# A graph layer with a gated update: layer norm of the second group on two engines, and a new order of work between the first and the second group

## Chip, core and metric

The kernel runs on one core of one Trainium2 chip, in one launch. The metric is the device time in microseconds (us). Engines are named as in the profile: PE is TensorE (PEld its weight loads), DVE is VectorE, ACT is ScalarE, POOL is GpSimd, and SP is SyncE, which here only issues transfers.

## What is computed

The inputs are 64 graphs of 128 nodes with 128 features and a 128x128 adjacency each. Cut to what matters:

```python
h = maximum(layernorm(x), 0)                       # per node
c = relu(bn1(conv1(h)))                            # 1x1 convolution over the nodes
x_conv = relu(bn2(conv2(c)) + h)                   # 17 taps, 128 -> 128 channels
s = h @ w_se.T + b_se                              # 3 numbers for each node
A = exp(-|s_n - s_m|^2) * adj
x_nmp = A @ relu(h @ w_msg.T + b_msg)              # messages, gathered
gi = concat([x_conv, x_nmp]) @ w_ih.T + b_ih       # gates r, z, n
gh = h @ w_hh.T + b_hh
r, z = sigmoid(gi_r + gh_r), sigmoid(gi_z + gh_z)
out = x + (1 - z) * tanh(gi_n + r * gh_n) + z * h
```

## The kernel before

The 64 graphs are worked on in 8 groups `g` of 8 graphs. A group has 1024 columns (8 graphs of 128 nodes), cut into two chunks `c` of 512. All products are float32 made of three matmuls on split numbers (`three`, lines 1016 to 1019: high times high, low times high, high times low); the high half of each operand is written by ACT, the low half by DVE. The 17 taps are done as nine smaller convolutions, `sub_conv(g, 0)` to `sub_conv(g, 8)`, on derived inputs `v_hi` and `v_lo` and on derived weights `wt_hi` and `wt_lo`, which the kernel makes itself during group 0 in 13 lots (`lot_high` on ACT, `lot_low` on DVE, line 694). Lot 12 holds the input weights of the gates.

There is no scheduler: each engine has one list of calls written by hand, and the engines meet at semaphores. The work of neighbouring groups is interlocked, and from group 1 on the lists are a loop. The order between groups 0 and 1 is written out. The names that matter there:

- Layer norm: `ln_stats(g)` (DVE, line 674, eight instructions) and `moments(g)` (line 681), then `ln_scale(g)` on POOL (lines 330 to 335: four small instructions, of which the power at 333 gives `rstd`), then `ln_rows(g)` on ACT (line 422, eight instructions, one a graph). For group 0 alone the split form is used: `ln_first` and `hn_rows_first` on DVE with four of the graphs (lines 706, 711, 714), `ln_scale_first` on POOL (324, only the power), and `ln_rows_first` on ACT with the other four (396).
- `h_transpose(g, c)` (PE, line 1036) turns the rows into `h`; ACT writes `h_hi` and `hf` (`h_rows`, 432 and 433) and DVE `h_lo` (`h_low`, 701). `by_graphs` (414) stores `h` once more, for the messages.
- `conv1` (PE), `conv1_rows` (ACT, 441, writes `cp`), and from `cp` on DVE `level2_b` (738), `level1`, `v_low_b`, `level2_u` and `v_low_u`.
- `messages(g)` on PE (1060 and 1063), on ACT (487 to 494). In the form for group 1 it uses PSUM banks 0 to 2 and so waits for `conv1_rows(1, 0)`, which empties bank 2. From its three numbers a node, `distances` makes `slots` (on POOL for every group but the first, lines 247 to 266), `factor_transposes` (PE, 1074), `factor_rows` (ACT, 500), `distance` (PE, 1087), `exponent` (ACT, 506) and `masked` (DVE, 819) follow, and last `gather` (PE, 1097), whose result ACT and DVE split into `n_hi` (514) and `n_lo` (825).
- Convolution results: `m_shared(g, i)` (ACT, 478) empties PSUM bank 0 after sub-convolutions 0, 3 and 6; the next of these on PE waits for it. `join_b`, `add_h`, `add_shared`, `join_y` (DVE, 776, 786, 797, 805) add up `y`, and `xc_high` (ACT, 520) and `xc_low` (DVE, 812) split it.
- Gates: `gates_h(g, c)` (nine matmuls on `h`, into banks 3, 4 and 6), `gates_in(g, c)` (nine on the gathered messages `n`, nine on `xc`). `ghn_rows` (526), `reset_rows` (532), `update_rows` (537), `candidate` (568) on ACT, `reset` (831, 835) and `update` (840 to 850) on DVE. In `gates_h(g, 1)` the part of gate z waits until `update_rows(g, 0)` has read bank 6:

```python
three(bank(4), HH(R), *h, True, False)
if c:
    pe.wait_ge(z_ready, NCH * g + 1)
three(bank(6), HH(Z), *h, True, False)
```

SP loads the rows `xin` of the next group once the last layer norm has read the buffer, then `xt`, stores the output, and loads the mask; it has one queue and waits in this order.

## Time and profile before

| | us |
|---|---|
| median of 3 runs | 298.87 |
| lowest and highest | 298.52, 299.6 |
| the profiled execution, its own time | 298.59 |
| its span, first to last instruction | 296.8 |
| PE busy in the span | 285.9 (96%) |
| DVE, ACT, POOL busy | 225.7, 185.9, 65.6 |

The span leaves 1.8 us of the execution's time outside it. The granted clock of PE is 0.998 of full speed over the span. In the rows below, a row of a timeline has the start, the duration, the engine, the line, what it writes and reads, and in brackets the idle time before it and what ended that. Durations of matmuls overlap: a matmul with 512 columns lasts some 0.40 us in the rows, while the next one starts about 0.23 us after it.

### The profile page before, as it was taken

The page shows a single profiled execution, that of the slowest core. Times are in us where ns is not written, and L with a number is a line of the kernel's source. Part 1 is how long each engine was busy: PE and PEld are TensorE (multiplying, and loading weights), DVE is VectorE, ACT ScalarE, POOL GpSimd, SP SyncE. Part 2 cuts the span into 40 slices and gives each one's busy share as a digit, 9 for nine tenths or more (in the row PEclk, how much of TensorE's full clock was granted, in tenths as well). Part 3 has the DMA queues.
Part 4 walks back from the last instruction along what each step waited for, and adds up shares of the span by engine and source line. Part 5 has one row for each costly group of instructions (what it writes and reads, how often), then busy time and mean ns, then how long its engine had stood idle before and what let it go on. Part 6 is the DMA issues. An engine that isn't in the chain of part 4 may idle for free.

```text
span 296.8 us, 5432 instructions
## 1 busy us (share of the span) xinstructions
PE 285.9 (96%) x1943; PEld 259.1 (87%) x1943; DVE 225.7 (76%) x497; ACT 185.9 (63%) x355; POOL 65.6 (22%) x129
## 2 busy tenths in 40 slices
PE   8999888999999999999999999999999999999993
PEld 6699866899889998899889998899988998899993
DVE  5988967986679668796598776796587966786556
ACT  3795479658656677548757567647666586561354
POOL 6300130750015300550005500351005500130000
PEclk9999999999999999999999999999999999999999
DMA  7700111044000610035000620017000420013001
GB/s 254 278 3 0 35 51 58 0 144 145 0 0 3 227 59 0 0 110 176 2 0 0 183 103 1 2 35 249 1 2 1 141 73 0 3 22 122 0 1 71
DMA packets 6798, 18.96 MB, mean 64 GB/s; under 512 B 882, under 2 KB 1268, under 8 KB 6772
## 3 DMA queue, kind: packets, MB, share of 16 engines
q1 hardware_dynamic: 6624, 18.62, 19.0%
q8 instruction: 15, 0.25, 0.4%
q14 instruction: 11, 0.09, 0.1%
q10 hardware_dynamic: 148, 0.01, 0.0%
HBM read 14.43 MB, written 4.19 MB: 63 GB/s over the span
## 4 chain that ended last, share of the span: by engine, by line
PE 84%; DVE 7%; ACT 4%; POOL 2%; issue 1%; DMA 1%; DVEq 0%; ACTq 0%; POOLq 0%
PE ps L1017 23%; PE ps L1019 22%; PE ps L1018 22%; PE ps L1063 4%; PE ps L1097 4%; PE ps L1201 3%; PE ps L1036 2%; DVE wt_lo L694 2%; PE ps L1060 1%; PE ps L1074 1%; ACT wt_hi L390 1%; PE ps L1087 1%; ACT cp L441 1%; DMA out<-gate 1%; DVE stats L674 1%
## 5 line engine op out<-in xcount | busy, mean ns | idle before, releaser
L1017 PE MATMUL ps<-v_hi,wt_hi 128*128 128x256 f32 x320 | 92.8, 290 | 2.0 <-DVE v_lo L754 0.8
L1019 PE MATMUL ps<-v_hi,wt_lo 128*128 128x256 f32 x320 | 90.1, 281 | 0.0
L1018 PE MATMUL ps<-v_lo,wt_hi 128*128 128x256 f32 x320 | 89.7, 280 | 0.0
L1017 PEld LDWEIGHTS ps<-v_hi,wt_hi 128*128 128x128 f32 x320 | 60.2, 188 | 3.5 <-issue 2.7
L1018 PEld LDWEIGHTS ps<-v_lo,wt_hi 128*128 128x128 f32 x320 | 60.4, 189 | 0.3
L1019 PEld LDWEIGHTS ps<-v_hi,wt_lo 128*128 128x128 f32 x320 | 60.1, 188 | 0.0
L247 POOL CAST slots<-s_sb 128x48 fp32r<-128x48 f32 x7 | 2.2, 311 | 147.9 <-ACT s_sb L489 147.9
L422 ACT ACTIVATE hn<-xin,nmr,rstd 128x128 f32<-128x128 f32 x56 | 22.3, 482 | 14.7 <-POOL nmr L335 14.7
L1017 PE MATMUL ps<-h_hi,wt_hi 128*128 128x512 f32 (+1 forms) x67 | 26.2, 391 | 0.0
L1019 PE MATMUL ps<-h_hi,wt_lo 128*128 128x512 f32 (+1 forms) x67 | 25.8, 386 | 0.0
L1018 PE MATMUL ps<-h_lo,wt_hi 128*128 128x512 f32 (+1 forms) x67 | 25.8, 385 | 0.0
L797 DVE TENSOR_TENSOR y<-y,mbs 128x512 f32<-128x512 f32 x16 | 11.0, 690 | 15.6 <-ACT mbs L478 15.4
L1017 PE MATMUL ps<-n_hi,wt_hi 128*128 128x512 f32 (+1 forms) x51 | 20.1, 394 | 1.2 <-DVE wt_lo L694 1.2
L805 DVE SCALAR_TENSOR_TENSOR y<-ps,par,y 128x256 f32<-128x256 f32 x32 | 14.9, 482 | 8.1 <-PE ps L1019 7.1
L1018 PE MATMUL ps<-n_lo,wt_hi 128*128 128x512 f32 (+1 forms) x51 | 19.5, 383 | 0.0
L1018 PE MATMUL ps<-xc_lo,wt_hi 128*128 128x512 f32 (+1 forms) x51 | 19.5, 383 | 0.0
L1019 PE MATMUL ps<-n_hi,wt_lo 128*128 128x512 f32 (+1 forms) x51 | 19.5, 382 | 0.0
L1019 PE MATMUL ps<-xc_hi,wt_lo 128*128 128x512 f32 (+1 forms) x51 | 19.5, 382 | 0.0
L1017 PE MATMUL ps<-xc_hi,wt_hi 128*128 128x512 f32 (+1 forms) x51 | 19.4, 380 | 0.0
L812 DVE SCALAR_TENSOR_TENSOR xc_lo<-y,xc_hi 128x512 fp32r<-128x512 f32 x16 | 10.3, 688 | 10.2 <-ACT xc_hi L520 10.2
L526 ACT ACTIVATE gn<-ps,par 128x512 f32<-128x512 f32 x15 | 10.4, 691 | 11.8 <-PE ps L1019 11.7
L514 ACT ACTIVATE n_hi<-ps 128x512 fp32r<-128x512 f32 x16 | 9.6, 599 | 13.0 <-PE ps L1097 13.0
(152 smaller groups left out, 647.9 us busy)
## 6 DMA issues: line engine op xcount, KB each, us to landing
mask<-adj_t SPq DMA_DIRECT2D x8, 512.0 KB, 3.3
xt<-x_t SPq DMA_DIRECT2D x8, 512.0 KB, 4.1
out<-gate SPq DMA_DIRECT2D x15, 256.0 KB, 4.1
xin<-x_nm SPq DMA_DIRECT2D x7, 512.0 KB, 3.8
w<-w_conv SPq DMA_DIRECT2D x1, 576.0 KB, 6.0
gate<-w_gate SPq DMA_DIRECT2D x1, 576.0 KB, 7.0
xin<-x_nm SPq DMA_DIRECT2D x2, 256.0 KB, 3.0
w<-w_conv SPq DMA_DIRECT2D x1, 512.0 KB, 5.0
```

The source lines that it names most:

```text
L422: last = act.activation(hn[:, j, :], xin[:, j, :], ACT.Identity, bias=nmr[:, j:j + 1], scale=rstd[:, j:j + 1])
L514: act.activation(n_hi[:, :, 4 * c:4 * c + 4], bank(src).rearrange("p (b n) -> p n b", n=P), ACT.Copy).then_inc(n_hi_ready, 1)
L526: act.activation(gn[c][:], bank(3), ACT.Identity, bias=par[:, HN:HN + 1], scale=0.5).then_inc(ghn_ready, 1)
L797: dve.tensor_tensor(y_at(s), y_at(s), mbs[1 + s][:].rearrange("p (l b) -> p l b", b=GB).unsqueeze(2).broadcast_to([P, QUART, 2, GB]), ALU. ...
L805: dve.scalar_tensor_tensor(out=at, in0=quarter(1 + t), scalar=par[:, SC2:SC2 + 1], in1=at, op0=ALU.mult, op1=ALU.add).then_inc(y_ready, 1)
L812: dve.scalar_tensor_tensor(out=xc_lo[:, cols(c)], in0=y[:, cols(c)], scalar=0.0, in1=xc_hi[:, cols(c)], op0=ALU.max, op1=ALU.subtract).the ...
L1017: pe.matmul(dst, wt_hi[:, blk, :], hi, start=start, stop=False)
L1018: pe.matmul(dst, wt_hi[:, blk, :], lo, start=False, stop=False)
L1019: return pe.matmul(dst, wt_lo[:, blk, :], hi, start=False, stop=stop)
L1063: last = pe.matmul(ps[:, first + k, i * MW:(i + 1) * MW], hg[:, 3 * k + i, :], w_a[:, P:P + MW], start=False, stop=i == count - 1)
L1097: last = pe.matmul(ps[:, dst, i * P:(i + 1) * P], msg[:, b, :], aff[:, b, :], start=True, stop=True)
L1201: pe.matmul(bank(4), idle[:, 0:P], idle[:], start=True, stop=True)
```

## The change

The layer norm of group 1 takes the split form that only group 0 had: DVE writes `vpe`, POOL makes only the power, DVE writes `nmr` and normalizes four graphs, ACT the other four. The helpers get the group as an argument, with waits for the last readers of their buffers. The lists between the groups are reordered:

- PE: `gates_in` becomes `gates_n` and `gates_xc`. `gates_h(0, 1)` comes ahead of the transposes of group 1, `gates_n(0, 1)` behind them and ahead of `conv1`, `messages(1)` ahead of `gates_xc(0, 1)`. In group 1, `factor_transposes` and `distance` come two sub-convolutions later.
- DVE: lot 12 and `n_low` come ahead of the `join_y` calls, `moments(1)` behind them. `update(0, 0)` comes ahead of `h_low(1, 0)`. `ln_stats(2)` moves up from the loop to behind `h_low(1, 1)`. At the head of group 1, `join_b` and `add_h` come ahead of `update(0, 1)`.
- ACT: `reset_rows(0, 0)`, then the four rows of layer norm, then `update_rows(0, 0)` and `candidate(0, 0)`, all ahead of `h_rows(1)`. `ghn_rows(0, 1)` comes behind `conv1_rows(1)`. In group 1, `m_shared(1, 0)` comes ahead of `factor_rows(1)`.

Groups 2 to 7 keep their order.

```diff
@@ -280,8 +281,8 @@
                 if g + 1 < NG:
 
                     sp.wait_ge(hn_ready, NCH * (g + 1))
-                    if g == 0:
-                        sp.wait_ge(hn_first, 1)
+                    if g < 2:
+                        sp.wait_ge(hn_first, g + 1)
                     sp.dma_start(xin[:], x_nm[g + 1]).then_inc(x_landed, 16)
 
                 upto(sp, sum_ready, NCH * g)
@@ -319,19 +320,24 @@
             pool.memset(slots[:, 0, :, 14:16].bitcast(F32), 1.0).then_inc(pool_set, 1)
             pool.memset(slots[:, 1, :, 12:14].bitcast(F32), 1.0).then_inc(pool_set, 1)
 
-            def ln_scale_first():
-                pool.wait_ge(vpe_first, 1)
+            def ln_scale_first(g):
+                pool.wait_ge(vpe_first, g + 1)
+
+                upto(pool, hn_ready, NCH * g)
+                upto(pool, hn_first, g)
                 pool.tensor_tensor(rstd[:], vpe[:], neg_half[:], ALU.pow).then_inc(rstd_first, 1)
 
             def ln_scale(g):
                 pool.wait_ge(mv_ready, g + 1)
 
                 upto(pool, hn_ready, NCH * g)
+                if g == 2:
+                    pool.wait_ge(hn_first, 2)
                 pool.tensor_scalar(vpe[:], mv[:, :, 1], EPS, None, ALU.add).then_inc(pool_ln, 1)
                 pool.tensor_scalar(nmean[:], mv[:, :, 0], -1.0, None, ALU.mult).then_inc(pool_ln, 1)
-                pool.wait_ge(pool_ln, 3 * g - 1)
+                pool.wait_ge(pool_ln, 3 * (g - 1) - 1)
                 pool.tensor_tensor(rstd[:], vpe[:], neg_half[:], ALU.pow).then_inc(pool_ln, 1)
-                pool.wait_ge(pool_ln, 3 * g)
+                pool.wait_ge(pool_ln, 3 * (g - 1))
                 pool.tensor_tensor(nmr[:], nmean[:], rstd[:], ALU.mult).then_inc(rstd_ready, 1)
 
             def two(i):
@@ -358,12 +364,13 @@
 
             pool.wait_ge(pool_set, 5)
             affine_power()
-            ln_scale_first()
+            ln_scale_first(0)
             affine()
-            for g in range(NG):
-                if g + 1 < NG:
-                    ln_scale(g + 1)
-                    distances(pool, g + 1)
+            ln_scale_first(1)
+            distances(pool, 1)
+            for g in range(2, NG):
+                ln_scale(g)
+                distances(pool, g)
 
         @block.scalar
         def _(act):
@@ -389,9 +396,11 @@
                     act.wait_ge(wg_landed, 16)
                 act.activation(wt_hi[:, first:first + count, :], source, ACT.Copy).then_inc(wt_hi_ready, 1)
 
-            def ln_rows_first():
-
-                act.wait_ge(rstd_ready, 1)
+            def ln_rows_first(g):
+
+                act.wait_ge(rstd_ready, g + 1)
+
+                upto(act, ht_ps, NCH * g)
                 for j in range(4, GB):
                     last = act.activation(hn[:, j, :], xin[:, j, :], ACT.Identity, bias=nmr[:, j:j + 1],
                                           scale=rstd[:, j:j + 1])
@@ -572,7 +581,7 @@
             act.wait_ge(row_ready, 2)
             act.activation(row[0:1, :], row_raw[0:1, :], ACT.Copy).then_inc(row_split, 1)
             act.activation(row_hi[32:33, :], row_raw[32:33, :], ACT.Copy).then_inc(row_split, 1)
-            ln_rows_first()
+            ln_rows_first(0)
             h_rows_first()
             lot_high(1)
             lot_high(2)
@@ -606,17 +615,17 @@
             act.wait_ge(pool_par, 8)
             ghn_rows(0, 0)
             xc_high(0)
-            ln_rows(1)
             reset_rows(0, 0)
+            ln_rows_first(1)
             update_rows(0, 0)
+            candidate(0, 0)
             h_rows(1, 0, 0)
             h_rows(1, 1, 1)
-            candidate(0, 0)
             by_graphs(1, 0, 0)
             by_graphs(1, 1, 1)
-            ghn_rows(0, 1)
             conv1_rows(1, 0, 2)
             conv1_rows(1, 1, 7)
+            ghn_rows(0, 1)
             v_high_b(1, 0)
             v_high_b(1, 1)
             messages(1)
@@ -627,8 +636,12 @@
                 ahead = g + 1 < NG
                 update_rows(g - 1, 1)
                 candidate(g - 1, 1)
-                factor_rows(g)
-                m_shared(g, 0)
+                if g == 1:
+                    m_shared(g, 0)
+                    factor_rows(g)
+                else:
+                    factor_rows(g)
+                    m_shared(g, 0)
                 exponent(g)
                 if ahead:
                     ln_rows(g + 1)
@@ -701,13 +714,16 @@
                 dve.tensor_tensor(h_lo[g % 2][:, cols(c)], hf[g % 2][:, cols(c)], h_hi[g % 2][:, cols(c)],
                                   ALU.subtract).then_inc(h_lo_ready, 1)
 
-            def ln_first():
-                dve.wait_ge(mv_ready, 1)
+            def ln_first(g):
+                dve.wait_ge(mv_ready, g + 1)
                 dve.tensor_scalar(vpe[:], mv[:, :, 1], EPS, None, ALU.add).then_inc(vpe_first, 1)
 
-            def hn_rows_first():
-
-                dve.wait_ge(rstd_first, 1)
+            def hn_rows_first(g):
+
+                dve.wait_ge(rstd_first, g + 1)
+
+                upto(dve, ht_ps, NCH * g)
+                upto(dve, hn_ready, NCH * g)
                 dve.scalar_tensor_tensor(out=nmr[:], in0=mv[:, :, 0], scalar=-1.0, in1=rstd[:], op0=ALU.mult,
                                          op1=ALU.mult).then_inc(rstd_ready, 1)
                 for j in range(4):
@@ -893,14 +909,14 @@
                 last = stats_of(0, j)
             last.then_inc(stats_ready, 1)
             moments(0)
-            ln_first()
+            ln_first(0)
             lot_low(0)
             dve.wait_ge(row_split, 2)
             dve.wait_ge(row_landed, 32)
             dve.tensor_tensor(row[32:33, :], row_raw[32:33, :], row_hi[32:33, :], ALU.subtract).then_inc(row_split, 1)
             dve.wait_ge(w2a_landed, 16)
             dve.tensor_tensor(fb[:, 0:4, :], w2[:, 0:8:2, :], w2[:, 1:8:2, :], ALU.add).then_inc(sums_ready, 1)
-            hn_rows_first()
+            hn_rows_first(0)
             dve.wait_ge(w2b_landed, 16)
             dve.tensor_tensor(fb[:, 4:8, :], w2[:, 8:16:2, :], w2[:, 9:16:2, :], ALU.add).then_inc(sums_ready, 1)
             dve.wait_ge(sums_ready, 2)
@@ -941,19 +957,22 @@
             masked(0, 0)
             masked(0, 1)
             lot_low(11)
-            moments(1)
             add_shared(0, 1)
-            join_y(0, 1, 0)
+            lot_low(12)
             n_low(0, 0, 5)
             n_low(0, 1, 7)
+            join_y(0, 1, 0)
             join_y(0, 1, 1)
-            lot_low(12)
+            moments(1)
+            ln_first(1)
             xc_low(0, 0)
             xc_low(0, 1)
+            hn_rows_first(1)
             reset(0, 0)
+            update(0, 0)
             h_low(1, 0)
             h_low(1, 1)
-            update(0, 0)
+            ln_stats(2)
             level2_b(1, 0)
             level2_b(1, 1)
             level1(1)
@@ -965,13 +984,20 @@
             reset(0, 1)
             for g in range(1, NG):
                 ahead = g + 1 < NG
-                if ahead:
-                    ln_stats(g + 1)
+                if g == 1:
                     moments(g + 1)
-                update(g - 1, 1)
-                join_b(g, 0)
-                join_b(g, 1)
-                add_h(g)
+                    join_b(g, 0)
+                    join_b(g, 1)
+                    add_h(g)
+                    update(g - 1, 1)
+                else:
+                    if ahead:
+                        ln_stats(g + 1)
+                        moments(g + 1)
+                    update(g - 1, 1)
+                    join_b(g, 0)
+                    join_b(g, 1)
+                    add_h(g)
                 masked(g, 0)
                 masked(g, 1)
                 add_shared(g, 0)
@@ -1019,8 +1045,8 @@
                 return pe.matmul(dst, wt_lo[:, blk, :], hi, start=False, stop=stop)
 
             def h_transpose(g, c, dst):
-                if g == 0 and c == 0:
-                    pe.wait_ge(hn_first, 1)
+                if g < 2 and c == 0:
+                    pe.wait_ge(hn_first, g + 1)
                 else:
                     pe.wait_ge(hn_ready, NCH * g + c + 1)
                 if g == 1:
@@ -1144,9 +1170,8 @@
                     pe.wait_ge(z_ready, NCH * g + 1)
                 three(bank(6), HH(Z), *h, True, False)
 
-            def gates_in(g, c):
+            def gates_n(g, c):
                 nm = [n[:, c * HALF:(c + 1) * HALF, :] for n in (n_hi, n_lo)]
-                xc = (xc_hi[:, cols(c)], xc_lo[:, cols(c)])
                 if c == 0:
                     pe.wait_ge(n_lo_ready, NCH * g + NCH)
                     if g == 0:
@@ -1156,6 +1181,9 @@
                     pe.wait_ge(v_ready, NCH * g + 1)
                 three(bank(5), IH(N, 1), *nm, True, False)
                 three(bank(6), IH(Z, 1), *nm, False, False)
+
+            def gates_xc(g, c):
+                xc = (xc_hi[:, cols(c)], xc_lo[:, cols(c)])
                 pe.wait_ge(xc_lo_ready, NCH * g + c + 1)
                 three(bank(4), IH(R, 0), *xc, False, True).then_inc(r_ps, 1)
                 if g < NG - 1:
@@ -1228,22 +1256,30 @@
             gather(0, 0, 5)
             gather(0, 1, 7)
             gates_h(0, 0, True)
-            gates_in(0, 0)
+            gates_n(0, 0)
+            gates_xc(0, 0)
+            gates_h(0, 1, True)
             h_transpose(1, 0, 0)
             h_transpose(1, 1, 1)
-            gates_h(0, 1, True)
+            gates_n(0, 1)
             conv1(1, 0, 2)
             conv1(1, 1, 7)
             messages(1)
-            gates_in(0, 1)
+            gates_xc(0, 1)
             for g in range(1, NG):
                 ahead = g + 1 < NG
                 sub_conv(g, 0)
-                factor_transposes(g)
+                if g > 1:
+                    factor_transposes(g)
                 sub_conv(g, 1)
-                distance(g)
+                if g > 1:
+                    distance(g)
                 sub_conv(g, 2)
+                if g == 1:
+                    factor_transposes(g)
                 sub_conv(g, 3)
+                if g == 1:
+                    distance(g)
                 sub_conv(g, 4)
                 sub_conv(g, 5)
                 gather(g, 0, 5)
@@ -1259,11 +1295,13 @@
                 if ahead:
                     conv1(g + 1, 0, 0)
                     conv1(g + 1, 1, 7)
-                gates_in(g, 0)
+                gates_n(g, 0)
+                gates_xc(g, 0)
                 if ahead:
                     gates_h(g, 1, ahead)
                     messages(g + 1)
-                    gates_in(g, 1)
+                    gates_n(g, 1)
+                    gates_xc(g, 1)
                 else:
                     for p in (1, 2):
                         part_gates_h(p)
```

## Rows read from the trace of the kernel before

**Rows 1.** Busy time by stretch: stretch, its length, busy us (instructions) by engine, clock, DMA.

```profile
36.00:57.00 21.00, 18.70 (x98) 15.13 (x98) 16.48 (x29) 17.49 (x36) 7.38 (x11) 1.00 0.16 51
...
90.00:124.00 34.00, 34.00 (x236) 31.08 (x235) 25.97 (x57) 21.92 (x42) 8.08 (x16) 1.00 0.19 63
```

**Rows 2.** Timeline of PE from group 0 to group 1: start, duration, instruction, idle time.

```profile
38.24 0.40 PE L1019 MATMUL ps<-h_hi,wt_lo 128*128 128x512 f32 x1
39.81 0.47 PE L1017 MATMUL ps<-n_hi,wt_hi 128*128 128x512 f32 x1 [1.17 <-DVE wt_lo L694]
...
44.10 1.03 PE L1036 MATMUL ps<-ident,hn 128*128 128x128 f32 x8
44.89 0.48 PE L1017 MATMUL ps<-h_hi,wt_hi 128*128 128x512 f32 x1
...
49.82 0.75 PE L1060 MATMUL ps<-row,ones 128*128 128x396 f32 x3 [1.13 <-ACT cp L441]
...
52.12 0.48 PE L1017 MATMUL ps<-n_hi,wt_hi 128*128 128x512 f32 x1
...
58.55 0.66 PE L1074 MATMUL ps<-ident,slots 128*128 128x128 f32 x4 [0.21 <-POOL slots L266]
```

**Rows 3.** Timeline of PE in group 1: the first gather and sub-convolution 6.

```profile
67.80 1.05 PE L1097 MATMUL ps<-aff,msg 128*128 128x128 f32 x8
...
69.04 0.36 PE L1017 MATMUL ps<-v_hi,wt_hi 128*128 128x256 f32 x1
```

**Rows 4.** Timeline of DVE, group 0 first, then from group 0 to group 1.

```profile
8.04 1.11 DVE L714 TENSOR_SCALAR hn<-xin,mv,rstd 128x128 f32<-128x128 f32 x4
...
35.41 0.64 DVE L681 BATCH_NORM_AGGREGATE mv<-stats 128x2 f32<-128x6 f32 x8
...
37.13 1.28 DVE L825 TENSOR_TENSOR n_lo<-ps,n_hi 128x512 fp32r<-128x512 f32 x2
...
38.72 0.95 DVE L694 TENSOR_TENSOR wt_lo<-gate,wt_hi 128x768 fp32r<-128x768 f32 x1
39.58 1.29 DVE L812 SCALAR_TENSOR_TENSOR xc_lo<-y,xc_hi 128x512 fp32r<-128x512 f32 x2
...
47.58 0.69 DVE L840 TENSOR_TENSOR gate<-hf,gn 128x512 f32<-128x512 f32 x1
...
50.47 0.78 DVE L738 TENSOR_TENSOR vtb<-cp 128x264 f32<-128x264 f32 x2 [0.27 <-ACT cp L441]
...
58.05 1.64 DVE L674 BATCH_NORM_STATS2 stats<-xin 128x6 f32<-128x128 f32 x8
```

**Rows 5.** Timeline of ACT from group 0 to group 1.

```profile
38.84 1.15 ACT L520 ACTIVATE xc_hi<-y 128x512 fp32r<-128x512 f32 x2 [0.81 <-DVE y L805]
39.89 3.19 ACT L422 ACTIVATE hn<-xin,nmr,rstd 128x128 f32<-128x128 f32 x8
...
44.30 0.69 ACT L537 ACTIVATE gate<-ps,par 128x512 f32<-128x512 f32 x1 [0.65 <-PE ps L1019]
...
48.93 1.50 ACT L441 ACTIVATE cp<-ps,par 128x512 f32<-128x512 f32 x2
...
68.12 0.45 ACT L478 ACTIVATE mbs<-ps,par 128x256 f32<-128x256 f32 x1
```

**Rows 6.** Timeline of POOL: the power for group 1 and for group 2.

```profile
37.14 1.67 POOL L333 TENSOR_TENSOR rstd<-vpe,neg_half 128x8 f32<-128x8 f32 x1
...
61.73 1.95 POOL L333 TENSOR_TENSOR rstd<-vpe,neg_half 128x8 f32<-128x8 f32 x1
63.76 1.22 POOL L335 TENSOR_TENSOR nmr<-nmean,rstd 128x8 f32<-128x8 f32 x1
```

**Rows 7.** Transfers: SP's issue of group 2's rows, and issues by kind with us to landing.

```profile
43.10 0.33 SPq L285 DMA_DIRECT2D xin<-x_nm  x1
...
xin<-x_nm SPq DMA_DIRECT2D x1, 512.0 KB, 3.4
...
gate<-w_gate SPq DMA_DIRECT2D x1, 576.0 KB, 7.0
```

## Prediction

> **What bounds the kernel now.** I read the busy times by stretch first. In a stretch of the steady loop PE is busy for all of 34.00 us; between the groups 0 and 1 it is busy 18.70 of 21.00 us, so 2.30 us are idle [rows 1]. The reader is to see that PE sets the time, that the change touches no matmul, and that nothing can be won but PE's idle time in the one place that the change edits. Then PE's timeline there: 1.17 us before the n gates, for the weights of lot 12; 1.13 us before `messages(1)`, for `cp`; and 0.21 us before the factor transposes, for `slots` [rows 2]. What a stall costs is best read from starts. The 512-column matmuls start every 0.234 us: from 38.24 the next would start at 38.47, and started at 39.81, 1.34 late. The first one behind a stall or a switch takes 0.32 to the next, 0.08 more. `messages(1)` starts at 49.82; the six matmuls of `conv1` end their slots at 48.54, so 1.28 are lost. Fifteen matmuls of 256 columns at 0.118 take 1.78, so `sub_conv(1, 0)`, which starts at 52.12 + 0.32 + 17 x 0.234 = 56.42, is done at 58.18; the transposes at 58.55 are 0.37 late, 0.30 beyond a plain switch [rows 2]. All three together: 1.42 + 1.28 + 0.30 = 3.0 us at most.
>
> **The n gates of group 0.** DVE is free at 35.41, where `moments(1)` stood [rows 4]. Now come: `add_shared` (an instruction of 512 columns, 0.60 from start to start) to 36.01; lot 12, whose 0.95 us hold DVE for 0.86 (38.72 to 39.58), to 36.87; the two of `n_low`, 1.20 held, to 38.07, the second complete at 38.15 [rows 4]. DVE to PE took 0.14 us at the stall (39.67 to 39.81) [rows 2, 4]. So `n` and lot 12 are there at 38.29, before PE wants them at 38.47. The stall is gone: 1.42 us gained, by 0.18 us of cover.
>
> The price is `y`: two `join_y` follow, 0.40 each, complete at 38.94 instead of 38.80. `xc_high` starts 38.98 (38.84 before) [rows 5], its first half ends near 39.63, and `xc_low`, behind `moments(1)` (0.56) and `ln_first` (0.09 to 0.2), writes its first half 39.67 to 40.36. PE gets it at 40.50 and wants it at 38.47 + 2.11 = 40.58: no stall, with 0.08 us to spare. If it is late, that costs 0.1 or so.
>
> **`gates_h(0, 1)` right behind.** It starts at 42.69; the switch of order gives nothing by itself. Its z part is wanted 1.41 later, at 44.10, and needs `update_rows(0, 0)`. ACT: r is complete at 41.45, `reset_rows` holds ACT from 41.48 to 42.07 (0.59 for 0.69, as at 44.30). Next come the four rows of layer norm, which wait for POOL. `vpe` is complete at 39.70; the power takes 1.67 or 1.95 [rows 6], so `rstd` is there at 41.46 to 41.75, `nmr` 0.2 later, before ACT is free at 42.07. Four rows are half of 3.19 [rows 5], 1.57 held, to 43.64; then `update_rows` to 44.33, seen by PE (0.05, as `cp` complete at 49.77 and 49.82) at 44.38. PE waits 0.28 us. This is a new stall: before, the transposes stood in that gap.
>
> The four DVE rows take 1.11 [rows 4], from 41.6 to 42.6 (42.9 with the long power); `reset(0, 0)` follows, complete at 44.02 to 44.32; the tanh of `candidate` starts when `update_rows` lets ACT go, 44.23 to 44.35, and is complete some 0.75 later, at 45.0 to 45.1.
>
> **Transposes, n gates, `conv1`.** PE: z part 44.38 to 45.16, transposes 0.79 (44.10 to 44.89) to 45.95, n gates 0.32 + 8 x 0.234 to 48.14 [rows 2]. DVE: `update(0, 0)` is four instructions, 2.5 us held (47.58 to 50.1) [rows 4], now in front of `h_low(1, 0)`: 45.0 to 47.5, then `h_low` complete at 48.2 and seen at 48.33 to 48.45. A wait of 0.2 us. `conv1(1, 0)` is complete at +0.95; `conv1_rows` takes 0.84 for the first chunk (1.50 for both [rows 5]), so `cp` is there at 50.2 to 50.3, and `messages(1)` starts there, where PE has been free since 49.82 + 0.05. So 0.35 to 0.45 of the old 1.28 us stay. The reader is to see that `messages(1)` starts later than before (50.20 against 49.82), but with the n gates of chunk 1 already done.
>
> `messages` takes 2.30 (49.82 to 52.12) [rows 2], then only nine matmuls, 2.19, are left: `sub_conv(1, 0)` starts at 54.69 against 56.42. **Gain so far 1.7 us.**
>
> **Group 1's start.** The stall at `factor_transposes` goes, since two more sub-convolutions stand before it: 0.30 gained, 2.0 in all. `ln_stats(2)`, 1.64 us [rows 4], now lies ahead of `level2_b(1, 0)`, but DVE waits there for the second `cp` anyway: free at 48.7, `cp` complete at 50.8 (50.43 before). It needs group 2's rows. Their load is issued when the layer norm has read `xin`, 43.10 before, about 43.7 now, and lands 3.4 us later [rows 7], 47.1. The cover is 2.1 less 1.6, so 0.5 us; without it the chain to `v_lo` would be late by what overlaps. `moments(2)` is then free of `ln_stats(2)` and starts at 58.43 instead of 59.7: DVE's chain in front of it is 0.38 later with `cp`.
>
> What is next late is bank 0 before `sub_conv(1, 6)`. `m_shared(1, 1)` stands behind `ln_rows(2)` on ACT and ended at 68.57, 0.47 before the start at 69.04 [rows 3, 5]. PE would now be there at 67.0. The chain: `moments(2)` complete 59.07, POOL's four instructions from 59.15 (behind `distances(1)`, done at 58.9) for the old 4.5 us (to 64.98 [rows 6]) or, as for group 1, whose DVE neighbours were other ones, 3.6; eight rows 3.1; `m_shared` complete between 66.9 and 67.3. PE waits 0 to 0.3, I take 0.15. The other new order, `update(0, 1)` behind `add_h`, leaves `masked(1, 0)` complete at about 64.9, before `gather(1, 0)` at 67.80 - 2.0 = 65.8 [rows 3]: 0.7 us of cover; if `candidate(0, 1)` were over 0.5 us later, it and bank 0 before `sub_conv(1, 3)` would cost the excess. SP's `xt` and stores move with `update(0, 1)` by about 1.5 us; the next user of each is over 10 us away.
>
> **Sum.** 1.70 + 0.30 - 0.15 = 1.85 us of the profiled execution's 298.59 us (296.8 span, 1.8 outside): 296.75. The median of the runs lies 0.28 above that execution, so I predict 297.0.
>
> **A rule weighed.** POOL's power took 1.67 beside `n_low` and 1.95 beside instructions of `update` with two inputs in SBUF, while the latter kept their 0.69 [rows 4, 6]. That the POOL side stretches agrees with a rule of the Trainium skill, "SBUF — State Buffer", section "Summary: rules for kernel authors": of a DVE instruction with two SBUF inputs and a GpSimd instruction that reads SBUF, the one issued second is blocked until the first is done. The new power starts at 39.8 beside the first `xc_low`; by that rule the second `xc_low` would wait for it. That is the rival priced third below.
>
> **Rivals.**
> 1. Everything is hidden: `update_rows` and `h_low` come in time, `cp` too. For it: each new stall is short. Against it: ACT's list has no room before 44.3. It gives 298.87 - 2.8 = 296.1 (3.0 less the switches). Chance 0.07.
> 2. The new covers (0.08, 0.18, 0.5, 0.5 us) are too thin, and waits of ACT and DVE add up behind PE: `reset_rows(0, 1)`, `candidate(0, 1)` and `m_shared(1, 0)` come 0.5 to 1 us late, and `sub_conv(1, 3)` or `(1, 6)` waits. The gain falls to 0.5 to 1.4: 297.5 to 298.4. For it: `cp` is 0.38 us later while PE is 2 us earlier. Chance 0.24.
> 3. POOL's power holds up DVE: `xc_low(0, 1)` waits until 41.5 and ends at 42.2, `hn_rows_first` starts 0.6 to 0.9 late, and with it `reset`, `candidate`, `update`, `h_low` and `conv1`. The gain falls by that, to 1.1: 297.8. Against it: no DVE instruction beside a power is longer in the rows. Chance 0.04.
> 4. Slower: group 2's rows land late, and `ln_stats(2)` blocks DVE ahead of all of group 1's convolution inputs. It costs one for one when they land later than 49.8, 6.1 us behind the issue (0.5 to `cp`, 0.5 more to `sub_conv(1, 3)`), takes the whole gain at 51.6, 7.9 us, and more than 0.5% at 53.1: 300.5. For it: a load of 576 KB took 7.0 us [rows 7], but at the start and behind five others; this one has the queues alone. Chance 0.05 for this side.
>
> My own forecast, gain 1.4 to 2.2, has 0.60. About 0.5%, 1.5 us, is what a measurement of this kernel can tell from no change: 297.4. Most of my forecast (0.54) and rival 1 lie below it: faster 0.61. The rest of it, rivals 2 and 3: same 0.35; slower 0.04. The range runs from 296.1 to 298.4; the likeliest case alone is 296.7 to 297.5.
>
> **What would show it.** PE: n gates at 38.5 without a wait; a wait of 0.2 to 0.4 in `gates_h(0, 1)` for `update_rows`; one of 0.1 to 0.3 at `conv1(1, 0)` for `h_low`; `messages(1)` near 50.2 for `cp`; `sub_conv(1, 0)` near 54.7; no wait at the transposes of group 1; `gather(1, 0)` near 65.8; a wait of at most 0.3 before `sub_conv(1, 6)`. DVE's `ln_stats(2)` between 48.7 and 50.4. From group 2 on every start earlier by the same 1.85. I would be wrong if a wait stands where I have none: at `gates_xc(0, 0)` for `xc_low`, or at `sub_conv(1, 3)` for `mbs`.

## The result, and the profile after

The changed kernel takes 296.84 us (median of 4 runs, 296.6 to 297.07) beside 299.02 us for the kernel before. The ratio is 0.993, 95% interval 0.9916 to 0.9944, so 1.7 to 2.5 us less. The profiled execution took 296.6 us, with a span of 294.8 against 296.8. Some executions of three kernels below (d2, d3 and d5) ran at a granted clock of 0.994 or less over the span instead of 0.996 or more, and took some 1 to 2 us longer than the others of the same kernel; all the traces come from executions at 0.995 or more.

Executions differ in when group 0 gets going, by more than some of the terms at stake. So the traces are compared over one stretch: from PE's first gate matmul of group 0 (`gates_h(0, 0)`) to its first of group 1. These are the two ends in the kernel before, and between them the start of `sub_conv(1, 0)`, timeline of PE:

```profile
36.29 0.48 PE L1017 MATMUL ps<-h_hi,wt_hi 128*128 128x512 f32 x1
...
56.40 0.28 PE L1017 MATMUL ps<-v_hi,wt_hi 128*128 128x256 f32 x1
...
74.72 0.40 PE L1017 MATMUL ps<-h_hi,wt_hi 128*128 128x512 f32 x1
```

It is 38.43 us long. PE's timeline after the change, with both ends; these rows answer to [rows 2, 3] (L1043 to L1045 are the three matmuls, before L1017 to L1019):

```profile
36.16 0.48 PE L1043 MATMUL ps<-h_hi,wt_hi 128*128 128x512 f32 x1
...
38.36 0.40 PE L1043 MATMUL ps<-n_hi,wt_hi 128*128 128x512 f32 x1
...
43.73 0.40 PE L1045 MATMUL ps<-h_hi,wt_lo 128*128 128x512 f32 x1
44.26 0.50 PE L1043 MATMUL ps<-h_hi,wt_hi 128*128 128x512 f32 x1
...
47.80 0.40 PE L1045 MATMUL ps<-n_hi,wt_lo 128*128 128x512 f32 x1
48.36 0.50 PE L1043 MATMUL ps<-h_hi,wt_hi 128*128 128x512 f32 x1 [0.17 <-DVE h_lo L714]
...
50.20 0.75 PE L1086 MATMUL ps<-row,ones 128*128 128x396 f32 x3 [0.17 <-ACT cp L450]
...
54.68 0.28 PE L1043 MATMUL ps<-v_hi,wt_hi 128*128 128x256 f32 x1
...
59.65 0.60 PE L1100 MATMUL ps<-ident,slots 128*128 128x128 f32 x4
...
65.62 1.05 PE L1123 MATMUL ps<-aff,msg 128*128 128x128 f32 x8
66.51 0.60 PE L1062 MATMUL ps<-ident,hn 128*128 128x128 f32 x4
67.06 0.36 PE L1043 MATMUL ps<-v_hi,wt_hi 128*128 128x256 f32 x1
...
72.73 0.40 PE L1043 MATMUL ps<-h_hi,wt_hi 128*128 128x512 f32 x1
```

The stretch is 36.57 us: 1.86 us shorter. The two profiled executions differ by 1.99 us; the other 0.13 is the earlier start of the stretch. The reader is to see that the three old waits are gone or small, and that four new ones, each of 0.2 to 0.33 us, stand in their place: before the z part (44.26 where 43.97 was due), before `conv1` (48.36, due 48.03), before `messages(1)` (50.20, due 49.87), and before `sub_conv(1, 6)` (0.55 behind the transposes instead of 0.35). Only two of them carry a releaser in the timeline: a row's bracket shows idle time behind the end of the last matmul, which lies some 0.16 us behind its slot, so a short wait is seen only in the starts.

What ACT, POOL and DVE did meanwhile, timelines after the change:

```profile
41.97 1.66 ACT L405 ACTIVATE hn<-xin,nmr,rstd 128x128 f32<-128x128 f32 x4
43.53 0.67 ACT L546 ACTIVATE gate<-ps,par 128x512 f32<-128x512 f32 x1
...
62.45 1.03 ACT L515 ACTIVATE aff<-ps 128x1024 f32<-128x1024 f32 x1 [1.56 <-PE ps L1113]
63.37 3.18 ACT L431 ACTIVATE hn<-xin,nmr,rstd 128x128 f32<-128x128 f32 x8
```

```profile
39.66 2.08 POOL L328 TENSOR_TENSOR rstd<-vpe,neg_half 128x8 f32<-128x8 f32 x1 [29.89 <-DVE vpe L719]
...
59.20 0.25 POOL L336 TENSOR_SCALAR vpe<-mv 128x8 f32<-128x8 f32 x1 [0.58 <-DVE mv L694]
...
59.86 1.67 POOL L339 TENSOR_TENSOR rstd<-vpe,neg_half 128x8 f32<-128x8 f32 x1
61.61 0.40 POOL L341 TENSOR_TENSOR nmr<-nmean,rstd 128x8 f32<-128x8 f32 x1
```

```profile
39.52 1.30 DVE L828 SCALAR_TENSOR_TENSOR xc_lo<-y,xc_hi 128x512 fp32r<-128x512 f32 x2
41.77 0.17 DVE L727 SCALAR_TENSOR_TENSOR nmr<-mv,rstd 128x8 f32<-128x8 f32 x1 [0.95 <-POOL rstd L328]
...
47.62 1.29 DVE L714 TENSOR_TENSOR h_lo<-hf,h_hi 128x512 fp32r<-128x512 f32 x2
48.83 1.64 DVE L687 BATCH_NORM_STATS2 stats<-xin 128x6 f32<-128x128 f32 x8
```

### The profile page after: what moved, and what is told of

Its sections match the earlier page's. It is cut to its first block, busy times and chain, and to the rows that moved or that the text cites. A ratio compares the mean times of both kernels' runs of the same rounds, so it can differ in the third digit from the quotient of the medians.

```text
span 294.8 us, 5433 instructions
## 1 busy us (share of the span) xinstructions
PE 285.8 (97%) x1943; PEld 258.7 (88%) x1943; DVE 226.9 (77%) x503; ACT 184.4 (63%) x351; POOL 61.7 (21%) x126
## 4 chain that ended last, share of the span: by engine, by line
PE 81%; issue 11%; DVE 3%; DMA 2%; ACT 2%; POOL 1%; SPq 0%; DVEq 0%; POOLq 0%
PE ps L1043 23%; PE ps L1045 22%; PE ps L1044 22%; PE ps L1089 4%; PE ps L1123 4%; PE ps L1062 2%; DMA w_a<-w_in 1%; PE ps L1086 1%; PE ps L1100 1%; PE ps L1113 1%; POOL rstd L328 1%; DMA out<-gate 1%; ACT hn L405 1%; DVE hn L730 0%; DVE gate L896 0%
## 5 line engine op out<-in xcount | busy, mean ns | idle before, releaser
L1043 PE MATMUL ps<-v_hi,wt_hi 128*128 128x256 f32 x320 | 92.8, 290 | 1.9 <-DVE v_lo L770 0.8
L1045 PE MATMUL ps<-v_hi,wt_lo 128*128 128x256 f32 x320 | 90.1, 281 | 0.0
L1043 PEld LDWEIGHTS ps<-v_hi,wt_hi 128*128 128x128 f32 x320 | 60.2, 188 | 3.6 <-issue 2.8
L1045 PEld LDWEIGHTS ps<-v_hi,wt_lo 128*128 128x128 f32 x320 | 60.1, 188 | 0.0
L248 POOL CAST slots<-s_sb 128x48 fp32r<-128x48 f32 x7 | 1.6, 227 | 147.3 <-ACT s_sb L498 147.3
L431 ACT ACTIVATE hn<-xin,nmr,rstd 128x128 f32<-128x128 f32 x48 | 19.1, 481 | 12.1 <-POOL nmr L341 12.1
L1043 PE MATMUL ps<-h_hi,wt_hi 128*128 128x512 f32 (+1 forms) x67 | 26.3, 392 | 0.3 <-DVE h_lo L714 0.2
L1045 PE MATMUL ps<-h_hi,wt_lo 128*128 128x512 f32 (+1 forms) x67 | 25.8, 386 | 0.0
L1043 PE MATMUL ps<-n_hi,wt_hi 128*128 128x512 f32 (+1 forms) x51 | 20.0, 392 | 0.0
L1045 PE MATMUL ps<-xc_hi,wt_lo 128*128 128x512 f32 (+1 forms) x51 | 19.5, 382 | 0.0
L1045 PE MATMUL ps<-n_hi,wt_lo 128*128 128x512 f32 (+1 forms) x51 | 19.5, 382 | 0.0
L1043 PE MATMUL ps<-xc_hi,wt_hi 128*128 128x512 f32 (+1 forms) x51 | 19.5, 382 | 0.0
```

The costliest lines, as they stand in the source:

```text
L431: last = act.activation(hn[:, j, :], xin[:, j, :], ACT.Identity, bias=nmr[:, j:j + 1], scale=rstd[:, j:j + 1])
L1043: pe.matmul(dst, wt_hi[:, blk, :], hi, start=start, stop=False)
L1045: return pe.matmul(dst, wt_lo[:, blk, :], hi, start=False, stop=stop)
```

## Experiments: one part of the change at a time

Ratios are to the kernel before, run beside each on the same chip; the stretch is that of the trace, gates to gates.

| | ratio (95%) | stretch, us |
|---|---|---|
| before | 1 | 38.43 |
| the changed kernel | 0.993 (0.9916 to 0.9944) | 36.57 |
| d1_n_early_only | 0.9994 (0.998 to 1.0008) | 38.30 |
| d2_no_split | 1.0042 (1.0022 to 1.0063) | 38.76 |
| d3_old_pe_order | 1.0031 (1.0018 to 1.0044) | 38.66 |
| d4_stats_late | 0.9941 (0.9926 to 0.9956) | 36.90 |
| d5_transposes_early | 1.0029 (1.0013 to 1.0045) | 38.95 |
| d6_rows_land_late | 0.9961 (0.9945 to 0.9978) | 37.41 |

**d1_n_early_only**, the kernel before with DVE's earlier supply of `n` and lot 12 alone:

```diff
             add_shared(0, 1)
-            join_y(0, 1, 0)
+            lot_low(12)
             n_low(0, 0, 5)
             n_low(0, 1, 7)
+            join_y(0, 1, 0)
             join_y(0, 1, 1)
-            lot_low(12)
```

> The kernel before with one part of the change: DVE's lot 12 and both n_low ahead of the join_y calls. moments(1) and the unsplit layer norm stay where they were. My theory (a chain through ACT holds group 1 back, so the first wait's end is given back): the n gates start near 38.9 instead of 39.81, PE then waits up to 0.6 us at the transposes for the last four rows of the layer norm (ACT: 40.6 to 43.7), messages(1) starts at 49.7 as before, the time is 298.7 to 299.0. Rival (each wait of PE counts by itself): 0.9 us faster, 298.1.

Its timelines of PE and of ACT:

```profile
36.81 0.48 PE L1017 MATMUL ps<-h_hi,wt_hi 128*128 128x512 f32 x1
...
39.27 0.50 PE L1017 MATMUL ps<-n_hi,wt_hi 128*128 128x512 f32 x1
...
43.66 1.33 PE L1036 MATMUL ps<-ident,hn 128*128 128x128 f32 x8
...
50.21 0.74 PE L1060 MATMUL ps<-row,ones 128*128 128x396 f32 x3 [1.13 <-ACT cp L441]
```

```profile
41.10 3.18 ACT L422 ACTIVATE hn<-xin,nmr,rstd 128x128 f32<-128x128 f32 x8
44.19 0.66 ACT L532 ACTIVATE gate<-ps,par 128x512 f32<-128x512 f32 x1
```

The n gates start 2.46 us after the stretch's start instead of 3.52, so 1.06 us of stall are gone. `messages(1)` starts 13.40 us after it instead of 13.53: 0.13 us are left. ACT's eight rows hold everything of group 1 until 44.2. PE's earlier start was paid back at the transposes and at `messages(1)`. Part of that is a price of this edit itself: with `moments(1)` still ahead of them, the `join_y` calls end later, and with `y` and `xc_high` ACT's rows begin 4.29 us after the stretch's start instead of 3.60.

**d2_no_split**, the changed kernel with the unsplit layer norm of group 1:

```diff
-            ln_scale_first(1)
+            ln_scale(1)
...
-            ln_rows_first(1)
+            ln_rows(1)
...
-            ln_first(1)
...
-            hn_rows_first(1)
```

The pieces are of POOL, of ACT, and two of DVE; the waits of SP, POOL and PE for the split form go too.

> The changed kernel with the unsplit layer norm of group 1: four instructions on POOL and eight rows on ACT, at the same places in the lists. My theory: POOL is done at 43.0, ACT's rows at 46.2, update_rows(0, 0) and with it the z part of gates_h(0, 1) come 2.6 us later than in the changed kernel (44.26 there), all behind is late by about 2.5 us, the time is 299.0 to 299.5: without the split the new order gains nothing. Rival (the split is off the path, the order does it): 296.8 to 297.3.

```profile
42.90 3.19 ACT L429 ACTIVATE hn<-xin,nmr,rstd 128x128 f32<-128x128 f32 x8 [0.82 <-POOL nmr L339]
45.99 0.67 ACT L544 ACTIVATE gate<-ps,par 128x512 f32<-128x512 f32 x1
```

PE then waits 2.56 us at the z part, and the stretch is 2.19 us longer than in the changed kernel, 0.33 longer than before the change. The split is what lets the new order pay. The ratio of 1.0042 holds more than that: eight of the ten executions ran at a granted clock of 0.990 or 0.991 and took 300.4 to 301.22 us; the other two, at 0.997 and 0.996, took 298.82 and 299.09. No trace of the former was kept, so why their clock was lower stays open.

**d3_old_pe_order**, the changed kernel with PE's old order:

```diff
-            gates_h(0, 1, True)
             h_transpose(1, 0, 0)
             h_transpose(1, 1, 1)
-            gates_n(0, 1)
+            gates_h(0, 1, True)
             conv1(1, 0, 2)
             conv1(1, 1, 7)
             messages(1)
+            gates_n(0, 1)
```

> The changed kernel with PE's old order: transposes ahead of gates_h(0, 1), and gates_n(0, 1) behind messages(1). My theory: conv1(1, 0) is held by h_low, which is behind update(0, 0), at 48.3 as in the changed kernel, and messages(1) by cp at 50.2; the nine matmuls of the n gates now stand behind instead of in that gap, so sub_conv(1, 0) starts at 56.7 instead of 54.68, and the time is 298.8. Rival (the gain is the earlier supply by DVE, the order on PE is worth little): under 297.5.

```profile
43.44 1.31 PE L1062 MATMUL ps<-ident,hn 128*128 128x128 f32 x8 [0.29 <-DVE hn L730]
...
48.78 0.50 PE L1043 MATMUL ps<-h_hi,wt_hi 128*128 128x512 f32 x1 [1.92 <-DVE h_lo L714]
```

PE waited 0.29 us for `hn`, 1.92 us for `h_lo` at `conv1`, and 0.17 us for `cp`. The stretch is 2.09 us longer than in the changed kernel, as expected. The nine matmuls of `gates_n(0, 1)` take those 2.1 us; they lie in the gap only in the new order.

**d5_transposes_early**, the changed kernel with `factor_transposes(1)` and `distance(1)` two sub-convolutions earlier, as before (and `factor_rows(1)` ahead of `m_shared(1, 0)`):

```diff
                 sub_conv(g, 0)
-                if g > 1:
-                    factor_transposes(g)
+                factor_transposes(g)
                 sub_conv(g, 1)
...
                 sub_conv(g, 2)
-                if g == 1:
-                    factor_transposes(g)
```

> The changed kernel with factor_transposes and distance of group 1 back behind the first and the second sub-convolution (and factor_rows ahead of m_shared(1, 0) on ACT). Theory of the prediction's text (this move is worth the 0.3 us stall of the kernel before): 0.3 us slower than the changed kernel. What the trace of the changed kernel now makes me expect: slots are ready at 58.63, sub_conv(1, 0) ends at 56.46, so PE waits 2.2 us, and the stretch from gates to gates is 38.5 instead of 36.57 us, the time 298.8: the move carries as much as the whole change, since the nine n gates that stood behind messages(1) are gone from there.

```profile
37.15 0.48 PE L1039 MATMUL ps<-h_hi,wt_hi 128*128 128x512 f32 x1
...
59.66 0.66 PE L1096 MATMUL ps<-ident,slots 128*128 128x128 f32 x4 [2.06 <-POOL slots L267]
...
76.10 0.40 PE L1039 MATMUL ps<-h_hi,wt_hi 128*128 128x512 f32 x1
```

The wait of 0.21 us [rows 2] is now 2.06 us, and the stretch is 2.38 us longer than in the changed kernel: the one part whose removal costs most.

**d4_stats_late**, the changed kernel with `ln_stats(2)` back at the head of group 1:

```diff
-            ln_stats(2)
...
                 if g == 1:
+                    ln_stats(g + 1)
                     moments(g + 1)
```

> The changed kernel with ln_stats(2) back at the head of group 1. My theory: DVE's 1.64 us push moments(2), POOL's layer norm, ACT's eight rows and m_shared(1, 1) back; sub_conv(1, 6) starts near 68.1 instead of 67.06, gather(1, 0) may wait 0.3 us for masked; the time is 297.8 to 298.1. Rival (the early statistics only fill an idle gap of DVE and nothing waits for them): 296.8.

```profile
66.58 1.16 PE L1123 MATMUL ps<-aff,msg 128*128 128x128 f32 x8 [0.23 <-DVE aff L835]
```

```profile
61.44 0.26 POOL L336 TENSOR_SCALAR vpe<-mv 128x8 f32<-128x8 f32 x1 [2.25 <-DVE mv L694]
...
63.85 0.20 POOL L341 TENSOR_TENSOR nmr<-nmean,rstd 128x8 f32<-128x8 f32 x1
```

It cost 0.33 us; I had put it at some 1.1. On the clock of this trace `gather(1, 0)` was due at 66.18 and started 0.40 us late, for `masked` (0.23 in the bracket), PE lost 0.11 more behind it, and the wait of 0.20 us at `sub_conv(1, 6)` was gone in return. So DVE's list carries the cost, not ACT's rows: POOL's four instructions took 2.61 us here, not the 3.6 to 4.5 that I had carried over from the kernel before, and ACT's rows began only 0.16 us later in the stretch than in the changed kernel.

**d6_rows_land_late**, the changed kernel with a load ahead of group 2's rows:

```diff
+                    if g == 1:
+                        sp.dma_start(extra[:], x_nm[3]).then_inc(extra_landed, 16)
+                        sp.wait_ge(extra_landed, 16)
                     sp.dma_start(xin[:], x_nm[g + 1]).then_inc(x_landed, 16)
```

> The changed kernel with group 2's rows landing late: SP first loads 512 KB into a buffer that nobody reads and waits for it, so that the rows land near 50.6 instead of 47.1. Theory (rival 4 of the prediction: it costs one for one from a landing at 49.8 on, through ln_stats(2) ahead of all convolution inputs of group 1): the rows' statistics end at 52.3, the convolution inputs are 1.35 us late, PE waits at sub_conv(1, 3), and the stretch from gates to gates is 37.4 to 37.7 us instead of 36.57. Against it: if the statistics had a place elsewhere on the path, all 3.5 us would show; if none of it was on the path, nothing would.

Its timelines of DVE and of POOL:

```profile
51.70 1.65 DVE L692 BATCH_NORM_STATS2 stats<-xin 128x6 f32<-128x128 f32 x8 [1.31 <-DMA xin<-x_nm]
53.26 0.76 DVE L759 TENSOR_TENSOR vtb<-cp 128x264 f32<-128x264 f32 x2
...
57.39 0.70 DVE L783 TENSOR_TENSOR v_lo<-u,v_hi 128x528 fp32r<-128x528 f32 x1
58.19 1.36 DVE L787 TENSOR_TENSOR v_lo<-vtu,v_hi 128x528 fp32r<-128x528 f32 x2
```

```profile
54.91 3.27 POOL L250 CAST slots<-s_sb 128x48 fp32r<-128x48 f32 x1 [11.69 <-ACT s_sb L503]
```

This execution began its stretch at 37.63, so 51.70 is 50.23 on the clock of the changed kernel's trace. The stretch grew by 0.84 us, inside what was expected, but not where: 0.75 us of it stand before the factor transposes (61.87, 24.24 us into the stretch instead of 23.49), for `slots`, of which 0.58 show as a wait. A cast of POOL that takes 0.23 us in the changed kernel took 3.27. On one clock `slots` are ready 1.72 us later than in the changed kernel (61.82 here, 58.63 there): 0.33 of it because POOL's first cast could start only then, behind ACT, and 1.39 because POOL's chain of eleven instructions took 6.91 us instead of 5.52. PE had some 1 us of cover there, so by this sum ACT's part alone would have cost nothing.

## Experiments: where the remaining waits come from

| | ratio (95%) | stretch, us |
|---|---|---|
| after_again | 0.9941 (0.9926 to 0.9955) | 36.57 |
| x1_act_interleaved | 0.9924 (0.9905 to 0.9942) | 36.56 |
| x2_h_low_earlier | 0.9919 (0.9902 to 0.9935) | 36.26 |
| x3_both | 0.9926 (0.9911 to 0.9941) | 36.42 |
| x4_all | 0.9919 (0.9903 to 0.9935) | 36.12 |
| x5_all_and_more | 0.9905 (0.9888 to 0.9921) | 35.67 |

**after_again** is the changed kernel once more.

> The changed kernel once more, as the measure for the three that run beside it: 296.8.

Its median was 297.34 us beside 299.11. Its execution began the stretch at 37.16, a whole microsecond later than the first, and the stretch has the same 36.57 us: the stretch repeats to 0.01 us where the start does not.

**x1_act_interleaved** splits ACT's four rows around `update_rows(0, 0)` (`ln_rows_half(1, 4)` makes the rows of graphs 4 and 5, `ln_rows_half(1, 6)` those of 6 and 7):

```diff
             reset_rows(0, 0)
-            ln_rows_first(1)
+            ln_rows_half(1, 4)
             update_rows(0, 0)
+            ln_rows_half(1, 6)
             candidate(0, 0)
```

> The changed kernel with update_rows(0, 0) between the first two and the last two of ACT's layer norm rows, and nothing else. My theory (the chain v_ready, candidate(0, 0), update(0, 0), h_low(1, 0) holds conv1, whatever PE does before): the wait at the z part of gates_h(0, 1) goes, the one before conv1(1, 0) grows by the same 0.3 us, and from PE's first gates of group 0 to its first gates of group 1 it stays 36.57 us (within 0.1). Rival (each wait of PE counts by itself): 36.3 us.

```profile
45.81 1.03 PE L1073 MATMUL ps<-ident,hn 128*128 128x128 f32 x8
...
49.51 0.50 PE L1054 MATMUL ps<-h_hi,wt_hi 128*128 128x512 f32 x1 [0.55 <-DVE h_lo L725]
```

The wait at the z part went, the one at `conv1` grew from 0.17 to 0.55 us in the bracket, and the stretch did not move. So a wait of PE that a later one swallows is not on the path.

**x2_h_low_earlier** puts `h_low(1, 0)` ahead of the last instruction of `update(0, 0)`, where the new argument of `update` is called:

```diff
-            update(0, 0)
-            h_low(1, 0)
+            update(0, 0, lambda: h_low(1, 0))
             h_low(1, 1)
```

> The changed kernel with h_low(1, 0) ahead of the last instruction of update(0, 0) on DVE. My theory: conv1(1, 0) is held by h_low alone; it now starts at 48.03 without a wait instead of 48.36, messages(1) and all behind start 0.3 us earlier: 296.5. Rival (conv1 or cp is held by ACT: h_rows, by_graphs): no change, 296.8.

```profile
48.21 0.39 PE L1044 MATMUL ps<-h_hi,wt_hi 128*128 128x512 f32 x1
```

The stretch began at 36.34, so `conv1(1, 0)` starts 11.87 us into it instead of 12.20, without a wait. The stretch is 0.31 us shorter, as expected: `conv1(1, 0)` was held by DVE's list alone.

**x3_both** has both edits.

> The same, and on ACT update_rows(0, 0) between the first two and the last two rows of layer norm. My theory: the z part of gates_h(0, 1) loses its wait of 0.3 us, and since h_low no longer waits for update(0, 0), conv1 starts at 47.7; messages(1) at 49.6, 0.6 us earlier than in the changed kernel: 296.2. Rival (h_low is still behind update's first three instructions, 47.6): no more than 0.3 to 0.4 us, 296.4 to 296.5.

It is 0.15 us shorter than the changed kernel, and longer than x2 alone. My theory fell; the rival was nearer. The second `h_low` was still behind `update`, and with it the second `conv1`; `m_shared(1, 0)`, behind `candidate(0, 1)`, became late for `sub_conv(1, 3)`:

```profile
49.53 0.50 PE L1055 MATMUL ps<-h_hi,wt_hi 128*128 128x512 f32 x1 [0.24 <-DVE h_lo L725]
...
60.54 0.36 PE L1055 MATMUL ps<-v_hi,wt_hi 128*128 128x256 f32 x1 [0.25 <-ACT mbs L497]
```

**x4_all** adds the r part of `gates_xc(0, 1)` ahead of `messages(1)`, and `m_shared(1, 1)` ahead of `ln_rows(2)`.

```diff
+            gates_xc_r(0, 1)
             messages(1)
-            gates_xc(0, 1)
+            gates_xc(0, 1, True)
...
                 exponent(g)
+                if g == 1:
+                    m_shared(g, 1)
                 if ahead:
                     ln_rows(g + 1)
-                m_shared(g, 1)
+                if g != 1:
+                    m_shared(g, 1)
```

> The same, and two more: on PE the r part of gates_xc(0, 1) (three matmuls, 0.7 us) ahead of messages(1), on ACT m_shared(1, 1) ahead of ln_rows(2) in group 1. My theory: the r part covers the wait of 0.33 us for cp, and sub_conv(1, 6) loses its 0.2 us wait for bank 0: 0.9 to 1.1 us faster than the changed kernel, 295.8. Rival (the chain behind cp, through v_lo, candidate(0, 1) and m_shared(1, 0), becomes the next to be late, at sub_conv(1, 3)): 296.1 to 296.3.

0.45 us shorter than the changed kernel, half of what I expected. The wait for the second `h_low` stayed: 0.23 us in the bracket, 0.40 by the starts (48.85, due at 48.45). The rival's place, `sub_conv(1, 3)`, cost 0.10 us.

**x5_all_and_more** takes the two causes that x3 showed away:

```diff
-            update(0, 0, lambda: h_low(1, 0))
-            h_low(1, 1)
+            update(0, 0, lambda: (h_low(1, 0), h_low(1, 1)))
...
                 update_rows(g - 1, 1)
+                if g == 1:
+                    m_shared(g, 0)
                 candidate(g - 1, 1)
                 if g == 1:
-                    m_shared(g, 0)
                     factor_rows(g)
```

> The version with everything: update_rows(0, 0) between ACT's rows, both h_low of group 1 ahead of the last instruction of update(0, 0), the r part of gates_xc(0, 1) ahead of messages(1), m_shared(1, 1) ahead of ln_rows(2), and m_shared(1, 0) ahead of candidate(0, 1). Theory: of the waits of x4_all, that for the second h_low (0.24) and that at sub_conv(1, 3) go; from gates to gates 35.8 to 35.9 us (x4_all: 36.12, the changed kernel 36.57), the time 0.7 to 0.8 below the changed kernel, 296.1. Rival (POOL's power, 2.08 us, holds the transposes and through v_ready all behind): 36.1, no better than x4_all.

```profile
36.77 0.48 PE L1058 MATMUL ps<-h_hi,wt_hi 128*128 128x512 f32 x1
...
50.44 0.65 PE L1101 MATMUL ps<-row,ones 128*128 128x396 f32 x3
...
59.49 0.66 PE L1115 MATMUL ps<-ident,slots 128*128 128x128 f32 x4
...
72.44 0.40 PE L1058 MATMUL ps<-h_hi,wt_hi 128*128 128x512 f32 x1
```

Timeline of POOL:

```profile
53.25 2.54 POOL L248 CAST slots<-s_sb 128x48 fp32r<-128x48 f32 x1 [10.90 <-ACT s_sb L508]
...
60.17 2.59 POOL L339 TENSOR_TENSOR rstd<-vpe,neg_half 128x8 f32<-128x8 f32 x1
```

The stretch is 35.67 us, a little less than the 35.8 to 35.9 expected, 0.90 shorter than the changed kernel's and 2.76 shorter than the one before. The median was 296.87 us beside 299.59. The traces put it ahead of the changed kernel. The interval of its ratio (0.9888 to 0.9921) overlaps a little with that of the changed kernel's first measurement (0.9916 to 0.9944) and not with that of its second (0.9926 to 0.9955), so the times alone leave the size of the gain less sure.

Something new stands in it: the factor transposes were due at 59.29 and started 0.20 us later, because `slots` were ready only at 59.43. POOL's cast took 2.54 us, as in d6 and in x4 (2.44).

## Why the prediction was right, and where a term was off

The forecast was a gain of 1.85 us and 297.0 us; the stretch gained 1.86, and the median was 296.84. The mechanism was right: PE's idle time in that place was the limit, and `update_rows`, `h_low`, `cp` and bank 0 were the next to be late. That the sums agree to 0.01 us is luck. At `sub_conv(1, 0)` the gain was 1.59 us (20.11 us into the stretch before, 18.52 after) where I had 1.7; from there to `gather(1, 0)` 0.46 us came on top where I had 0.30; and `sub_conv(1, 6)` took 0.20 where I had 0.15.

By its steps, with the predicted starts moved to the clock of the changed kernel's trace, which runs 0.13 us ahead of the one that I predicted from:

- **n gates** without a wait, predicted for 38.34, seen at 38.36. d1 shows that this part by itself gives 0.13 us, with a price on ACT that the changed kernel does not pay: the 1.42 of the sum exist only together with the others.
- **z part**: a wait of 0.28 us predicted, 0.29 seen. The path through ACT was right, but x1 shows that this wait is not on the path. I had it in PE's line of sums without harm, since the next step took the later of the two chains.
- **`conv1` and `messages(1)`**: 0.2 and 0.35 to 0.45 predicted, 0.33 and 0.33 seen; `messages(1)` predicted for 50.07, seen at 50.20. POOL's power took 2.08 us, longer than either of my bounds, and shifted `hn` and `reset` by 0.1 to 0.4, and with them `h_low`.
- **`sub_conv(1, 0)`** predicted for 54.56, seen at 54.68, late by what `messages(1)` was.
- **The factor transposes**: no wait, as said. As a difference of the two kernels the term was mis-sized: I had taken 0.07 us off the old lateness of 0.37 for a plain switch, and there is none (59.65 is just where the next matmul was due), and the sub-convolution behind follows in 0.35 us instead of 0.41; that makes 0.43. Nor is it a measure of what the move carries: d5 says 2.38 us. With nine matmuls fewer between `messages(1)` and the transposes, the old stall of 0.21 grows to 2.06 there.
- **`sub_conv(1, 6)`**: 0.15 us taken, 0.20 seen, for a partly wrong reason. I had ACT's eight rows wait for POOL until up to 63.7. POOL was done at 62.01, in 2.81 us instead of 3.6 to 4.5, and the rows began at 63.37, right behind `exponent`, which had moved back with `distance`. That is the mis-sized term: POOL's layer norm for group 2. It is also why the early statistics are worth 0.33 us (d4) and not 1.1. The lower end of my 66.9 to 67.3 for `m_shared` does not follow from POOL's 3.6 us either (62.75 + 3.1 + 0.45 is 66.3); that it was complete at 66.91 is the doing of `exponent`.
- **Rival 4**: rows that landed at 50.23, 50.36 on the clock of the prediction, cost 0.84 us, not the 0.56 of "one for one from 49.8". What failed is the place: not `sub_conv(1, 3)` was reached first, but `slots`. ACT's `v_high_b` waited for `vtb` ahead of `messages(1)` in its list (0.33 us of the 1.72), and POOL was held up (1.39, below).
- **The rule weighed**: rival 3, a power that holds up DVE, did not come. The two `xc_low` took 1.30 us beside the power against 1.29 [rows 4]. The loser was POOL, with 2.08 us against 1.67 for the power at 59.86; it took 2.07 or 2.08 in all eleven traces in which it started 0.14 or 0.15 us behind the first `xc_low`. The Trainium skill, "SBUF — State Buffer", section "Summary: rules for kernel authors", says that the one issued second is blocked; here the power was issued beside an `xc_low` that had begun 0.14 us earlier, and the next `xc_low` did not wait for it. So the trace agrees for POOL as the second, and not for DVE as the second.

## What to carry to other kernels

When one engine sets the time, sum its stalls by starts, not by brackets, and then ask of each whether a later one would swallow it: here one part alone gave 0.13 us, and each of three parts taken away cost the whole gain. A price for a part of a reordering is therefore only good together with the others; carry the order through as a schedule of all engines, as a list of "free at" and "ready at". In these traces small instructions of POOL have no fixed duration: price them by what DVE does beside them in the new order.

## What the hardware showed that I had not expected

POOL's small instructions stretch when they start during one of DVE's instructions with two inputs in SBUF: `nmr` took 1.22 us [rows 6], 0.40 in the changed kernel and 0.20 in d4. The amount is about what is left of DVE's instruction. In x5 the power started 0.16 us into `y<-hf,mb`, which takes 1.23 us, and lasted 2.59 us, 0.92 more than the 1.67 of other traces. In the changed kernel the same `y<-hf,mb` started during the power (60.72, the power from 59.86), and neither was longer than usual.

In d6 a cast of 48 elements a partition took 3.27 us: it began at 54.91, among DVE instructions of that kind that followed one another without a pause from 53.26 to 58.09, and ended at 58.18, when DVE had paused for ACT. In x4 and x5 it took 2.44 and 2.54 us and ended at 55.60 and 55.79, at the same pause; in the other eleven traces, within the same row of DVE instructions, it took 0.23 to 0.82. So such an instruction can be held over several of DVE's, not just one. What decides between the short and the long case these traces do not show. The Trainium skill, "SBUF — State Buffer", section "Summary: rules for kernel authors", has the loser fully blocked until the first finishes; the trace of d6 agrees with the blocking, and shows it lasting across five instructions and more, where the page ends it with the first.

The start of the stretch moved between 36.16 and 37.63 us from execution to execution, with the same work ahead of it. In the latest one DVE waited until 8.72 us for the first convolution weights, where it went on at 7.36 in the kernel before; medians of a few runs carry this scatter, the stretch does not.
